# A bridge between an expert block and attention: rotary partners by shuffle, combine on one engine, weight fold turned

## The reference

```
x = x + 0.5 * ffn(layernorm(x))      # 8 experts, each token goes to its best 2, weighted sum of their results
x = x + attn(layernorm(x))
x = x + 0.5 * ffn(layernorm(x))
```

```
q_lat = (x @ Wq_down).reshape(b, t, 16, 64)            # the same for k and v
q_c, q_e = q_lat @ Wq_up_c, q_lat @ Wq_up_e            # 8 + 8 columns a head
rot(x)[2i], rot(x)[2i+1] = -x[2i+1], x[2i]
q = concat(q_c, q_e * cos + rot(q_e) * sin)            # the same for k; v = v_lat @ Wv_up
att = softmax(causal(q @ k.T / 4));  x = x + (att @ v) @ Wc
```

## Time and profile before

| | |
|---|---|
| median of three runs | 1146.39 us (1146.26 to 1146.56) |
| profiled execution | 1147.94 us, span 1146.2 us, mean granted TensorE clock 0.908 |
| busy share of the span | TensorE 85%, VectorE 70%, ScalarE 55%, GpSimd 44% |
| the bridge | 289.8 to 416.85 us of the span |

### The profile page before, as it was taken

The page is one execution under the profiler, slowest core; times in us unless marked ns, Lnnn a source line. Parts: engine busy times, 40 slices in busy tenths (PEclk is TensorE's granted clock), DMA queues, the critical chain, the costliest instruction groups (busy, mean ns, idle before and its releaser), DMA issues. The chain is left out here.

```text
span 1146.2 us, 23328 instructions
## 1 busy us (share of the span) xinstructions
PE 972.9 (85%) x8630; PEld 719.1 (63%) x8630; DVE 806.1 (70%) x1689; ACT 631.5 (55%) x1445; POOL 499.7 (44%) x684
## 2 busy tenths in 40 slices
PE   5326999998899979999999999999886399999930
PEld 1125888887888855555555555555464388888830
DVE  3895655565577658888888988888628755655547
ACT  2733444443476525878787887878757534444410
POOL 1535777775546421223232332323211167777620
PEclk9757999999599986999999999999998589999975
DMA  8733565553548672346455553644229523333258
GB/s 302 238 122 109 201 220 203 211 197 131 184 150 247 186 199 57 85 102 151 102 121 116 123 123 85 135 99 104 59 67 341 180 94 104 103 105 103 97 177 299
DMA packets 100655, 172.82 MB, mean 151 GB/s; under 512 B 15873, under 2 KB 64513, under 8 KB 100545
## 3 DMA queue, kind: packets, MB, share of 16 engines
q1 hardware_dynamic: 86912, 134.09, 40.1%
q0 software_dynamic: 13632, 37.24, 9.8%
HBM read 101.55 MB, written 69.47 MB: 149 GB/s over the span
## 5 line engine op out<-in xcount | busy, mean ns | idle before, releaser
L1914 ACT ACTIVATE spare<-h_psS 128x512 f32<-128x512 f32 x576 | 306.5, 601 | 83.9 <-PE h_psS L1821 82.1
L1939 DVE TENSOR_REDUCE h_part<-h_psM 128x2 f32<-128x1024 f32 (+3 forms) x256 | 249.0, 1015 | 12.1 <-PE h_psM L1800 11.7
L1969 POOL TENSOR_SCALAR_AFFINE_SELECT spare<-spare 128x256 f32<-128x256 f32 x256 | 99.5, 407 | 293.8 <-ACT spare L1914 293.8
L929 PE MATMUL m_psG<-wgu,m_x_hi 128*128 x568 | 193.1, 421 | 1.7 <-DVE m_x_lo L1002 1.0
L1848 PE MATMUL h_psO<-spare,a_VP 128*17 128x256 f32 (+3 forms) x3072 | 163.6, 331 | 8.3 <-ACT spare L1902 7.3
L889 POOL DMA_INDIRECT ys<-m_y,m_slot_u x142 | 140.1, 986 | 59.4 <-issue 35.0
L883 POOL DMA_INDIRECT m_xg<-xn,m_slot_u x138 | 133.5, 967 | 47.9 <-issue 36.0
L1821 PE MATMUL h_psS<-h_QT,h_KT 49*128 49x512 f32 x720 | 149.0, 400 | 2.7 <-ACT spare L1914 2.7
L991 ACT ACTIVATE m_act_g<-m_psG 128x256 f32<-128x256 f32 x142 | 54.6, 384 | 142.7 <-PE m_psG L929 142.7
L1939 DVE TENSOR_REDUCE h_least<-h_psM 128x2 f32<-128x256 f32 (+3 forms) x128 | 99.6, 820 | 35.3 <-PE h_psM L1784 35.3
L1848 PEld LDWEIGHTS h_psO<-spare,a_VP 128*17 128x17 f32 x3072 | 79.6, 97 | 70.8 <-ACT spare L1902 17.0
(11 more groups left out here) (232 smaller groups left out, 1567.2 us busy)
## 6 DMA issues: line engine op xcount, KB each, us to landing
xn<-spare SPq DMA_DIRECT2D x16, 512.0 KB, 6.8
wg_d<-wgu SPq DMA_DIRECT2D x16, 512.0 KB
results<-ys SPq DMA_DIRECT2D x16, 512.0 KB, 5.2
a_KD<-spare SPq DMA_DIRECT2D x32, 256.0 KB, 3.0
a_OD<-spare SPq DMA_DIRECT2D x128, 64.0 KB, 2.5
wgu<-wg_d SPq DMA_DIRECT2D x16, 512.0 KB, 10.7
last<-ys SPq DMA_DIRECT2D x16, 512.0 KB, 7.1
h_KT<-a_KD SPq DMA_DIRECT2D x60, 132.0 KB
```

Of the source, the lines that this page charges most:

```text
L929: m = pe.matmul(out, s[:, c, :], ww[c], start=(n == 0), stop=(n == 3 * CC - 1))
L1914: act.activation(prob[k % NP][:, h, :], psS[x % NS][:, :], ACT.Exp).then_inc(s_read, 1)
L1939: m = dve.tensor_reduce(out, psM[k % NM][:, :, at:at + n], AX.X, ALU.max, negate=True)
L1969: m = pool.affine_select(block, block, [[0, 2], [1, P]], ALU.is_ge, 0.0, 0, -1)
```

## The change

Four things, all in the bridge.
- The packs ks and qs go. VectorE reads ke out of PSUM with a stream shuffle that exchanges neighbouring partitions (`SWAP`), into t2; it also makes the cosine product as before. GpSimd makes the sine product (new tile t3) and then the sum. Four packs now have one PSUM bank each.
- The products with the first expert's results move from ScalarE, and their sum from GpSimd, to VectorE: eight fused products per group there, four before. ScalarE's `first` and GpSimd's `add` go.
- The fold is the other way round: the small matrix is the stationary operand with 32 columns, the wide one moves with 256, and four heads' worth of results go to four groups of 32 output partitions (`multiply`). ScalarE copies them to SBUF (`copy_heads`), TensorE transposes them (`turn_heads`), and the rounding follows.
- The order in the first part: ScalarE rounds k's fold before group 0 is normalised, and VectorE splits group 0 before it combines group 1.

```diff
-PACKS = ("ke", "ks", "kc", "qe", "qs", "qc")
+SWAP = [n ^ 1 for n in range(32)]
+PACKS = ("ke", "kc", "qe", "qc")
...
+                def multiply(w):
+                    pe.wait_ge(down_in[w], 16)
+                    for q in range(2):
+                        for j in range(4):
+                            m = pe.matmul(head_ps[w][q][2 * DH * j:2 * DH * (j + 1), :], up[:, w, :], down[w][:, 4 * q + j, :],
+                                          start=True, stop=True)
+                        m.then_inc(multiplied, 1)
+                def turn_heads(i):
+                    w = FOLDS[CC * i][0]
+                    pe.wait_ge(copied, 2 * (i + 1))
+                    for c in range(CC):
+                        for q in range(2):
+                            m = pe.transpose(fold_ps[w][c][:, q * P:(q + 1) * P], head_sb[w][q][:, c * P:(c + 1) * P], ident[:, :])
+                        m.then_inc(folded, 1)
...
-                    dve.wait_ge(xs_done, g + 1)
+                    dve.wait_ge(y_in[g % NF], 32 * (g // NF + 1))
                     for a in range(PER):
                         t = PER * g + a
+                        dve.scalar_tensor_tensor(X[:, t, :], yg[0][g % NF][:, a, :], weight[:, 0, t:t + 1], X[:, t, :],
+                                                 ALU.mult, ALU.add).then_inc(x_half, 1)
+                    for a in range(PER):
+                        t = PER * g + a
+                        dve.wait_ge(x_half, t + 1)
                         dve.scalar_tensor_tensor(X[:, t, :], yg[1][g % NF][:, a, :], weight[:, 1, t:t + 1], X[:, t, :],
                                                  ALU.mult, ALU.add).then_inc(x_done, 1)
...
-                    for i, tile in enumerate((t1, t2)):
-                        q = NP * g + PACKS.index(k) + i
-                        dve.wait_ge(packed, q + 1)
-                        dve.tensor_tensor(tile[k][:, :], psP[q % 4][:, :], rope[:, i, at:at + HALF], ALU.mult
-                                          ).then_inc(p_read, 1)
+                    dve.stream_shuffle(t2[k][:, :], psP[q % 4][:, :], SWAP).then_inc(p_read, 1)
+                    dve.tensor_tensor(t1[k][:, :], psP[q % 4][:, :], rope[:, 0, at:at + HALF], ALU.mult
+                                      ).then_inc(p_read, 1)
...
+                    pool.wait_ge(p_read, 6 * g + READS[k] - 1)
+                    pool.tensor_tensor(t3[k][:, :], t2[k][:, :], rope[:, 1, at:at + HALF], ALU.mult).then_inc(spun, 1)
-                    pool.tensor_tensor(es[k][:, :], t1[k][:, :], t2[k][:, :], ALU.add).then_inc(summed, 1)
+                    pool.tensor_tensor(es[k][:, :], t1[k][:, :], t3[k][:, :], ALU.add).then_inc(summed, 1)
```

More of the change, by code:

```diff
@@ L1229, in project @@
         assert results.n == NF and results.W == PER
[L1230 removed]
+        XN = [place(f"XN{j}", 14 + j, [PER, C]) for j in range(2)]
         x_hi, x_lo = ([place(f"{n}{j}", i + j, [CC, HALF], F32R) for j in range(2)] for n, i in (("x_hi", 2), ("x_lo", 4)))
@@ L1341, in _ @@
                 pe.wait_ge(up_in, 16 * 2 * 5)
[L1343 to L1352, removed]
+                def multiply(w):
[12 more added lines that the diff above has]
+                        m.then_inc(folded, 1)
+                multiply(1)
+                multiply(0)
+                turn_heads(0)
+                turn_heads(1)
+                multiply(2)
                 pe.wait_ge(glo_done, 1)
@@ L1355, in _ @@
                 turn(0)
-                for w, c in FOLDS[2 * CC:]:
-                    fold_weights(w, c)
+                turn_heads(2)
                 pe.wait_ge(flo_done, 8)
-                pe.wait_ge(w_ready, 16)
                 for g in range(NG):
                     pe.wait_ge(xlo_done, 2 * g + 2)
-                    for n in range(3):
-                        pack(g, n)
+                    pack(g, 0)
+                    pack(g, 1)
                     if g + 1 < NG:
                         turn(g + 1)
[L1366 to L1370, removed]
+                    if g == 0:
+                        pe.wait_ge(flo_done, 10)
+                    value(g, 0)
+                    pack(g, 2)
+                    value(g, 1)
+                    pack(g, 3)
+                    value(g, 2)
                     value(g, 3)
@@ L1374, in _ @@
             def _(act):
[L1375 to L1380, removed]
-                        act.activation(part0[g % 2][:, a, :], yg[0][g % NF][:, a, :], ACT.Copy, scale=weight[:, 0, t:t + 1]
-                                       ).then_inc(part_done, 1)
                 def deviate(g):
@@ L1422, in value_out, with copy_heads, high_fold @@
                     act.activation(lx[:, n, 0:E], psV[n % 2][:, C:C + E], ACT.Copy, scale=std[:, g, a:a + 1]).then_inc(v_out, 1)
+                def copy_heads(i):
+                    w = FOLDS[CC * i][0]
+                    for q in range(2):
+                        act.wait_ge(multiplied, 2 * i + q + 1)
+                        act.activation(head_sb[w][q], head_ps[w][q], ACT.Copy).then_inc(copied, 1)
+                def high_fold(i):
+                    for n in range(CC * i, CC * (i + 1)):
+                        src, scale, (h, _) = fold(n)
+                        act.wait_ge(folded, n + 1)
+                        act.activation(h, src, ACT.Copy, scale=scale).then_inc(fhi_done, 1)
                 for k in range(CC):
-                    act.activation(w_eff[0][:, k, 4 * C:4 * C + E], middle[:, k, 0:E], ACT.Copy).then_inc(ghi_done, 1)
-                first(0)
+                    act.activation(w_eff[0][:, k, 3 * C:3 * C + E], middle[:, k, 0:E], ACT.Copy).then_inc(ghi_done, 1)
                 act.wait_ge(g_made, 1)
@@ L1594, in _ @@
                 pool.wait_ge(mask_made, 12)
-                add(0)
-                add(1)
-                pool.wait_ge(flo_done, 8)
-                for k, s in (("ke", "ks"), ("qe", "qs")):
-                    for w in w_eff:
-                        for c in range(CC):
-                            src, out = (w[:, c, BASE[n] * P:(BASE[n] + 1) * P].rearrange("p (g two) -> p g two", two=2)
-                                        for n in (k, s))
-                            for way in range(2):
-                                pool.tensor_copy(out[:, :, way], src[:, :, 1 - way]).then_inc(w_ready, 1)
-                add(2)
-                add(3)
+                pool.wait_ge(rope_in, 16)
                 for g in range(NG):
```

65 lines of the change are left out of this document (30 added, 35 removed).

## The result

The changed kernel takes 1154.51 us (median of six runs, 1150.94 to 1156.42) against 1146.33 us before (six runs, 1144.58 to 1147.2). The ratio is 1.0066, with a 95% interval of 1.0044 to 1.0088: slower by about 0.7%, 1.7 us above the 1152.8 predicted and inside the range. The profiled execution has a span of 1152.7 us, 6.5 more than before.

A forecast was written before the change was run, and what follows sets the result against it. A ring of waits through the in-order queues was taken as the bound, TensorE close behind. Terms -2.4, +10.4, -2.6 and +1 gave +6.4 us: 1154.3 for the profiled execution, median 1152.8, range 1144.5 to 1160.

The forecast's parts named there:

- The start, -2.4: Bridge start up to group 2's square root: 2.4 us shorter, as a VectorE and ScalarE chain takes most of 10.8.
- Signs at 304 and 317.5: Times in us expected in the changed profile: first projection product near 304, square root of group 2 near 317.5.
- the 14.3 us bound: Upper bound for the fold's 48 records on TensorE if column groups don't overlap; 6 us was taken.
- The ring, 14.9 us: Waits through the in-order queues from one square root to the next: 12.51 becomes 14.9 us, +10.4 over five.
- the tiny product's hold of 1.41: Steady ring: without GpSimd's 1024-column add, a tiny VectorE product is no longer held, -1.41 us a ring.
- Rotary, +0.76: Steady ring: one VectorE product less (-0.63), a GpSimd product more (+1.29), GpSimd's wait (+0.1): +0.76 us.
- Four more products and a collision, +3.07: Steady ring: four more VectorE combine products (+1.57), GpSimd's low part of qe landing in their run (+1.5).
- Rival B: Steady ring: VectorE keeps the port through its run, GpSimd waits; ring 13.4 us, total 1144.2 to 1147; 17%.
- Rival C: Steady ring: TensorE is the real bound there; faster by 3 to 9 us, 1137 to 1143; 13%.
- The last groups, -2.6: Last three groups, without combine: 32.7 us with TensorE the bound becomes 30.1, so -2.6.
- a term of its own: Last groups: 1 us added in case a slow TensorE clock stretch falls on them.
- rival D: Idle stretches keep TensorE's clock at half, or the fold costs 14.3 us: +10 to +22 us; 10%.

The follow-up runs named there:

- fold_only: Kernel before with only the new fold (column groups, then transposes) and the new order at the start; six packs and old combine stay: ratio 1.0037 to before.
- shuffle_only: Kernel before with only the stream shuffle, GpSimd's sine product and four packs; old fold and old combine stay: ratio 1.0022 to before.
- low_behind: Changed kernel with one wait more: GpSimd's low part of qe starts only after VectorE's eight combine products of group g+3: ratio 1.0013 to before.
- best_a: Changed kernel with queues reordered to open the ring of waits, old combine from group 3 on, expert-result load issued first: ratio 0.9980 to before.
- opened: Kernel before with VectorE's and ScalarE's work reordered to cut the ring of waits open, nothing else changed: ratio 0.9991 to before.
- combine_back: Changed kernel with the old combine put back (first products on ScalarE, add on GpSimd, four products on VectorE): ratio 1.0021 to before.

## Why the prediction was right

**The start, -2.4:** -2.12 by the start's length (27.93 against 30.05). Signs at 304 and 317.5 came at 303.86 and 317.17. The fold took 3.64 us for two matrices (4 said); the 14.3 us bound is out. That bound was also worked out too low: it took durations at full clock, where the pace counts, and the fold runs at half clock. The products of the second line of the earlier trace rows stand 0.43 us apart for 512 columns at a granted clock of 1.00 (row at the end of this document), which is 0.43 for 256 at half clock, so 20.6 us for 48 records, as an estimate. That the start is VectorE's and ScalarE's was right: the first projection product comes 11 us earlier, the square root of group 2 only 2.7. But I had taken the fold for a gain by itself, and fold_only shows none while the combine waits for GpSimd.

**The ring, 14.9 us:** 14.73 us on average, five of them +9.42 (+10.4 said). By its terms: the tiny product's hold of 1.41 went whole (0.14 us now). Rotary, +0.76, is +0.91 by shuffle_only's rings; the shuffle lasts 0.74 us, starts 0.63 before its successor, and the sine product and the sum stand 1.42 apart. So the shuffle came as taken (0.64), the sine product costs 1.42 where 1.39 was put, and the rest of the 0.15 is not placed. Four more products and a collision, +3.07: by low_behind the collision is 1.05 and not 1.5, the term that was mis-sized. The low part costs 1.04 in the ring shown (2.70 against 1.66) where I had put its full 1.3; the 0.2 for the end of the sum of qe wasn't there. The products themselves are 0.39 each, as said.

**Does GpSimd get in between two products?** Yes, once per product, as worked out from the earlier trace rows; best_a shows it with four in a row. Rival B (VectorE keeps its run whole) is out.

**Rival C (TensorE is the bound):** out for the changed kernel; TensorE stood 2.3 to 5.3 us in each ring, 3.9 on average where I had said about 5. The near tie in the kernel before was real: opened, its ring stops at 12.2 us.

**The last groups, -2.6:** -0.73 (32.01 against 32.74). This term failed. Windows of the stretch (columns as in the earlier trace rows):

```profile
390.80:396.00 5.20, 4.62 (x28) 3.74 (x26) 4.67 (x13) 2.67 (x6) 2.75 (x3) 1.00 0.26 73
396.00:402.00 6.00, 3.84 (x16) 3.55 (x17) 0.69 (x1) 4.51 (x14) 4.92 (x4) 0.74 0.53 156
402.00:408.00 6.00, 6.00 (x36) 5.23 (x35) 3.87 (x9) 2.66 (x7) 3.28 (x3) 0.97 0.88 236
```

After its last long stop (2.74 us) TensorE was granted 0.74 in one window, half clock for about half of it. In low_behind the clock is 1.00 there, and the rest takes 30.51, near my 30.1: 1.5 us for the clock. A second pair gives the same: combine_back has such a window (0.74) and a rest of 32.34, shuffle_only, which has the same code in these groups, has none and 30.80. The window row says so too: 6.00 us at 0.74 is the work of 1.56 us at full clock lost, with TensorE at work from 398.16 on. I had put 1 for it in a term of its own, so the two together are -0.7 against -1.6. In the rings the clock fell too, and there it cost nothing:

```profile
332.00:346.70 14.70, 12.36 (x76) 10.61 (x75) 11.16 (x29) 7.18 (x19) 7.88 (x6) 1.00 0.73 217
346.70:361.40 14.70, 9.68 (x49) 8.38 (x48) 11.13 (x29) 7.29 (x19) 7.86 (x6) 0.77 0.71 212
```

The two rings are 14.74 and 14.67 us long, at 1.00 and at 0.77; TensorE's slack covers it, as I had said. The sign that I had given for rival D, a clock under 0.8 in the steady part, did come: 0.77 in three of the five rings, 0.88 and 1.00 in the others. It was a bad sign, since rings at 0.77 are no longer than those at 1.00. Rival D wanted half clock throughout; the clock stood at 0.50 only for parts of a ring, and its price fell on the last groups alone. What I had not seen: in the last groups GpSimd is as late as TensorE. Its sine products of ke are at 403.79 and 413.31, 9.52 us apart, six operations and their waits.

**The sum:** +6.4 said for the profiled execution, +6.5 in its span. That it agrees within 0.2 us is luck: a ring smaller by 0.2 (five times) and a tail larger by 0.9 cancelled. The median came out 1.7 us above the forecast because I had taken 1.55 off the profiled execution's time, as for the kernel before; the profiled execution of the changed kernel, 1154.46 us, lies at its median. The two compared were 1154.3 said and 1154.46 measured.

## What to carry to other kernels

Price an instruction by what it does to the ring that passes through the in-order queues, and only then by its engine's busy share. When two engines block each other, as VectorE and GpSimd did here, a run of short instructions on the one pays for each long operation of the other that is ready beside it; put such a run where the other's queue is empty, and let work out of PSUM lie beside it. Opening the ring without that was worth 0.9 us of 14.7: the same work took 14.7, 13.9 and 11.65 us a ring in three orders.

## What the runs showed of the hardware

- VectorE's products with two SBUF inputs and GpSimd's operations take turns, one for one. A GpSimd operation of 1.3 us let into such a run lengthens it by 1.04 to 1.12 us (1.66 to 2.70 and to 2.78), three in a row of 1.47, 1.30 and 2.56 us by 4.5 (1.66 to 6.12). The Trainium skill, SBUF — State Buffer, on who interferes with whom, has the loser blocked for the whole of the other's instruction; the traces agree, with 1.04 to 1.12 us lost for 1.3, and add who comes next in a run.
- A wait added on GpSimd made the kernel's bridge 6.75 us shorter (low_behind): 5.26 in the rings, and 1.5 in the last groups, where the clock happened to be granted in full.
- A shuffle of 128x512 fp32 out of PSUM takes 0.74 us, and its successor starts 0.63 us after it, the pace of the products in the earlier trace rows (1.27 us for two).
- Four fp32 products of 256 columns in four column groups, weights of 32 columns each, took as long as one would: four records every 0.43 us at a granted clock of 0.50 (32 records in 3.64 us). For one alone, records of 512 columns stand 0.43 us apart at 1.00, from the trace of the kernel before, and twice the columns at twice the clock is taken as the same time:

```profile
24.48 1.89 PE L654 MATMUL m_psL<-spare,middle 128*8 128x512 f32 x4 [1.76 <-DMA spare<-x_turned]
```

- TensorE's clock fell and rose again within single rings. In the ring from 346.73 TensorE stood from 348.96 to 353.99; the granted clock was 1.00 until 351, 0.53 from 351 to 353, 0.50 to 0.51 (the level of 1.2 GHz) until 358, with TensorE at work from 353.99, and 1.00 (2.4 GHz) from 358 on. In the five rings, stops of 5.26, 2.34, 5.03, 3.30 and 3.76 us went with mean clocks of 0.77, 1.00, 0.77, 0.88 and 0.77.
